# An expert layer's sorted rows: 32x32 block transposes on VectorE in place of TensorE transposes in the tile loop

## What is computed

```
router_logits = x @ router_w.T                 # [1024, 8]
topk_vals, topk_ids = top_k(router_logits, 1)
gate = sigmoid(topk_vals)
xs = x * gate
for e in 8 experts:                            # wg 256x1024, wd 512x256
    g, u = split(xs @ wg[e])
    o = (silu(g) * u) @ wd[e]
    routed += where(topk_ids == e, o, 0)
shared = silu_mul(x @ shared_gate_up) @ shared_down
out = routed + shared
```

## Time and profile before

| | |
|---|---|
| median of 3 runs | 129.22 us (129.17 to 129.29) |
| profiled execution, its own time | 129.24 us |
| its span in the trace | 127.6 us |
| PE busy, share of the span | 122.1 us, 96% |
| PE weight loads | 106.1 us, 83% |
| DVE busy | 79.4 us, 62% |
| ACT busy | 53.4 us, 42% |
| POOL busy | 35.4 us, 28% |
| granted TensorE clock | full in every slice |

### The profile page before, as it was taken

How to read it: one execution, slowest core, us unless ns; L and a number is a source line. 1 busy time by engine, 2 the same in 40 slices (tenths; PEclk the granted TensorE clock), 3 DMA queues, 4 the chain that set the end, 5 groups by cost and what they waited for, 6 DMA issues and landing times.

```text
span 127.6 us, 2426 instructions
## 1 busy us (share of the span) xinstructions
PE 122.1 (96%) x822; PEld 106.1 (83%) x822; DVE 79.4 (62%) x175; ACT 53.4 (42%) x113; POOL 35.4 (28%) x65
## 2 busy tenths in 40 slices
PE   4989999999999999999999999999999999999990
PEld 1248776788888857999999999999999978999990
DVE  0799695997899999875575553505040428922471
ACT  1678796829987546322222222242221337200000
POOL 7804040003879300040303030303030301687500
PEclk9999999999999999999999999999999999999999
DMA  3784999999993210129797989888982031033437
GB/s 83 207 281 37 330 360 244 181 207 397 385 380 136 82 51 0 46 81 318 264 321 258 295 275 277 307 280 303 281 303 63 9 86 51 13 89 104 112 101 244
DMA packets 15748, 25.02 MB, mean 196 GB/s; under 512 B 1296, under 2 KB 12632, under 8 KB 15736
## 3 DMA queue, kind: packets, MB, share of 16 engines
q1 hardware_dynamic: 13368, 20.66, 53.1%
q0 software_dynamic: 1456, 3.41, 8.2%
q10 hardware_dynamic: 912, 0.80, 1.9%
HBM read 18.78 MB, written 6.08 MB: 195 GB/s over the span
## 4 chain that ended last, share of the span: by engine, by line
PE 80%; POOL 6%; issue 5%; DMA 4%; DVE 2%; ACT 0%; DVEq 0%; POOLq 0%
PE ps L1112 25%; PE ps L1126 13%; PE ps L300 6%; POOL q_sb L458 6%; PE ps L302 5%; PE ps L301 5%; PE ps L975 5%; PE ps L988 4%; PE ps L981 4%; PE ps L1066 4%; DMA q_sb<-sorted_rows,slot_row 2%; PE ps L1053 2%; DMA sorted_rows<-yrow 2%; PE ps L1060 2%; DVE x_sb L895 1%
## 5 line engine op out<-in xcount | busy, mean ns | idle before, releaser
L1112 PE MATMUL ps<-xgT,gu 128*128 128x144 f32 x256 | 34.2, 287 | 0.0
L1112 PEld LDWEIGHTS ps<-xgT,gu 128*128 128x128 f32 x256 | 32.3, 190 | 0.5 <-issue 0.2
L826 DVE TENSOR_TENSOR wqkv<-rz,ps 128x288 f32<-128x288 f32 x16 | 7.3, 454 | 25.5 <-ACT rz L576 25.5
L440 POOL DMA_DIRECT2D sorted_rows<-yrow x9 | 5.0, 558 | 54.7 <-DVE yrow L821 54.7
L1126 PE MATMUL ps<-wqkv,dn 128*128 128x144 f32 x128 | 17.4, 289 | 0.0
L576 ACT ACTIVATE rz<-ps 128x288 f32<-128x288 f32 x16 | 6.5, 409 | 25.0 <-PE ps L1112 25.0
L1126 PEld LDWEIGHTS ps<-wqkv,dn 128*128 128x128 f32 x128 | 16.1, 190 | 0.0
L432 POOL DMA_INDIRECT sorted_rows<-xn,slot_row x8 | 9.8, 1220 | 15.4 <-ACT xn L514 13.6
L300 PE MATMUL ps<-xT_hi,sgu_hi 128*128 128x512 f32 x32 | 13.0, 407 | 0.0
L301 PE MATMUL ps<-xT_lo,sgu_hi 128*128 128x512 f32 x32 | 12.6, 394 | 0.0
L302 PE MATMUL ps<-xT_hi,sgu_lo 128*128 128x512 f32 x32 | 12.6, 394 | 0.0
(11 more groups left out here) (162 smaller groups left out, 231.3 us busy)
## 6 DMA issues: line engine op xcount, KB each, us to landing
gu<-in_L_ffn_w_gate_up_dram SPq DMA_DIRECT2D x8, 1024.0 KB
dn<-in_L_ffn_w_down_dram SPq DMA_DIRECT2D x8, 512.0 KB
sorted_rows<-zeros SPq DMA_DIRECT2D x1, 2592.0 KB, 18.0
wqkv<-sorted_rows SPq DMA_DIRECT2D x10, 144.0 KB
sorted_rows<-yrow POOLq DMA_DIRECT2D x9, 128.0 KB, 2.1
sgu<-_ffn_shared_gate_up_dram SPq DMA_DIRECT2D x1, 1024.0 KB, 6.2
wqkv<-in_L_attn_w_qkv_dram SPq DMA_DIRECT2D x3, 256.0 KB, 3.7
x_sb<-in_L_attn_x_dram SPq DMA_DIRECT2D x2, 256.0 KB, 3.6
```

Of the source, the lines that this page charges most:

```text
L826: V.tensor_tensor(hr[:, 2 * h:2 * h + 2, :].rearrange("p f s -> p (f s)"), act_sb[:, h, 0:2 * SLOTS], ps[:, 2 * h + 1, 0:2 * SLOTS], ALU.m ...
L1112: ins = mm(ps[:, 2 * h + u, (f % 2) * SLOTS:(f % 2 + 1) * SLOTS], gu[p][:, kc, col:col + P], xgT[:, kc, :], start=(kc == 0), stop=(kc == K ...
```

## The change

The sorted rows are loaded so that feature 2 f + c of a slot sits in partition f, by four DMAs, one for each 32 partitions, with runs of 64 floats (256 bytes). One DVE transpose in blocks of 32x32 (`sorted_in`) makes `xgT` of them, with the even features in one chunk and the odd ones in the other. The gate and up weights are therefore loaded with rows 2 p and 2 p + 1 in partition p (one run of 8 KB instead of two of 4 KB), and the down weights are read with a step of two floats. Another DVE transpose (`rows_out`) reads the down projection's PSUM and writes `yrow`, from which four DMAs store with runs of 256 bytes. Since a tile is now moved as 160 rows of which 144 are its own, a tile's stores must land before those of the next begin; POOL waits for that. Both kinds of PE transposes, ACT's copies of `xgT` and `yT`, and the two DVE copies are gone. The last tile's four stores are issued two by POOL and two by SP.

```diff
-        xg = early[0:HS, 0:2 * D].rearrange("p (j d) -> p j d", j=2)
+        xg = early[:, 0:NSQ * SQ * KC].rearrange("p (j f) -> p j f", j=NSQ)
...
-        gu_dram = w_gate_up.rearrange("e (c p) n -> e p c n", p=P)
+        gu_dram = w_gate_up.rearrange("e (p c) n -> e p c n", c=KC)
...
+        def row_store(eng, t, b, q, s_store):
+            rows = sorted_rows[bass.ds(t * SLOTS, NSQ * SQ), q * SQ * KC:(q + 1) * SQ * KC]
+            eng.dma_start(rows.rearrange("(j p) f -> p j f", p=SQ), yrow[q * SQ:(q + 1) * SQ, b, :, :]).then_inc(s_store, 16)
...
         # SP
-            def sorted_load(t):
-                sp.dma_start(xg, sorted_rows[bass.ds(t * SLOTS + SLOTS, SLOTS), :].rearrange("(j p) d -> p j d", p=HS)).then_inc(s_xg, 16)
+            def sorted_load(first, s_load):
+                for q in range(P // SQ):
+                    rows = sorted_rows[bass.ds(first, NSQ * SQ), q * SQ * KC:(q + 1) * SQ * KC]
+                    sp.dma_start(xg[q * SQ:(q + 1) * SQ, :, :], rows.rearrange("(j p) f -> p j f", p=SQ)).then_inc(s_load, 16)
...
-                    sp.wait_ge(s_xgT, t + 2)
-                    sorted_load(t + 2)
+                    sp.wait_ge(s_xgc, t + 2)
+                    sorted_load(t * SLOTS + 3 * SLOTS, s_xg)
...
         # POOL
-            for t in range(E - 1):
-                row_store(t, t % 2)
+            for t in range(1, E - 1):
+                pool.wait_ge(s_yrow, t + 1)
+                if t >= 2:
+                    pool.wait_ge(s_ystore, 64 * (t - 1))
+                for q in range(P // SQ):
+                    row_store(pool, t, (t - 1) % 2, q, s_ystore)
...
         # ACT
-                sorted_copy(t + 2, 4)
-                act.wait_ge(s_down, t + 1)
-                A(yT[:, 0:KC * P].rearrange("p (c s) -> p c s", c=KC), ps[:, 5:7, 0:P], ACT.Copy)
-                A(yT[:, KC * P:].rearrange("p (s c) -> p c s", c=KC), ps[:, 5:7, P:SLOTS], ACT.Copy).then_inc(s_yT, 1)
...
         # DVE
+            def sorted_in():
+                V.transpose(xgT[:, :, :], xg.rearrange("p j (f c) -> p c j f", c=KC)).then_inc(s_xgc, 1)
...
             for k in range(LAST):
+                if k == LAST - 1:
+                    dve.wait_ge(s_xg0, 64)
+                    sorted_in()
                 hidden(k)
...
+            def rows_out(t, b, stored):
+                dve.wait_ge(s_down, t)
+                if stored is not None:
+                    dve.wait_ge(s_ystore, stored)
+                V.transpose(yrow[:, b, :, :].rearrange("p j (f c) -> p c j f", c=KC), ps[:, 5:7, 0:NSQ * SQ]).then_inc(s_lastrow if t is total else s_yrow, 1)
...
+            def expert_tile(t, b=None, stored=None):
+                if b is not None:
+                    rows_out(t, b, stored)
                 for h in range(2):
                     dve.wait_ge(s_silu, 2 * t + (h + 1))
...
-                    if h == 0:
-                        rows_copy(t, b, stored)
+                dve.wait_ge(s_xg, 64 * t + 64)
+                dve.wait_ge(s_gup, 2 * t + 2)
+                sorted_in()
...
         # PE
                         ins.then_inc(s_gup, 1)
-                        if h == 0:
-                            pe.wait_ge(s_yrow, t + 1)
-                            transpose_back(t + 1)
+                    pe.wait_ge(s_yrow, t + 1)
                     if e == 0:
                         pe.wait_ge(s_sh, LAST)
-                    transpose_sorted(4, s_xg, 16 * t + 16)
...
-                                ins = mm(ps[:, 5 + c, 0:SLOTS], dn[p][:, f, c * P:(c + 1) * P], hr[:, f, :],
+                                ins = mm(ps[:, 5 + c, 0:SLOTS], dn[p][:, f, :].rearrange("p (m c) -> p c m", c=KC)[:, c, :], hr[:, f, :],
```

More of the change, by code:

```diff
@@ L19 @@
 SLOTS = 144
-HS = SLOTS // 2
-REST = SLOTS - 128
+SQ = 32
+NSQ = (SLOTS + SQ - 1) // SQ
 WARM = 14
@@ L138, in build @@
         dn = [sb(f"dn{p}", [P, FC, D], F32) for p in range(2)]
[L139 to L142, removed]
+        xgT = sb("xgT", [P, KC, NSQ * SQ], F32)
+        yrow = sb("yrow", [P, 2, NSQ, SQ * KC], F32)
         early = wqkv[:, :, :].rearrange("p c n -> p (c n)")
-        xg = early[0:HS, 0:2 * D].rearrange("p (j d) -> p j d", j=2)
+        xg = early[:, 0:NSQ * SQ * KC].rearrange("p (j f) -> p j f", j=NSQ)
         hr = early[:, 2 * D:2 * D + FC * SLOTS].rearrange("p (f s) -> p f s", f=FC)
@@ L266, in build @@
         s_down = sem("s_down")
-        s_yT = sem("s_yT")
-        s_yback = sem("s_yback")
         s_yrow = sem("s_yrow")
-        s_ystore = [sem(f"s_ystore{b}") for b in range(2)]
+        s_ystore = sem("s_ystore")
         s_stored = sem("s_stored")
-        s_lastrest = sem("s_lastrest")
-        s_restdone = sem("s_restdone")
+        s_lastrow = sem("s_lastrow")
+        s_ylast_sp = sem("s_ylast_sp")
+        s_ylast_pool = sem("s_ylast_pool")
         s_gather = [sem(f"s_gather{i}") for i in range(NT)]
@@ L368, in _ @@
                 rows_of(e)
-            sp.wait_ge(s_xg, 16 * ends[7] + 16)
-            sp.wait_ge(s_lastrest, 1)
-            sp.dma_start(sorted_rows[bass.ds(ends[7] * SLOTS + P, REST), :].rearrange("s (c d) -> (s c) d", c=KC), yrest[:, 0, :]).then_inc(s_restdone, 16)
+            sp.wait_ge(s_xg, 64 * ends[7] + 64)
+            sp.wait_ge(s_lastrow, 1)
+            sp.wait_ge(s_stored, 1)
+            for q in range(2, P // SQ):
+                row_store(sp, ends[7], 1, q, s_ylast_sp)
             for i in range(1, NT, 2):
@@ L436, in _ @@
             total = pool.value_load(plan[0:1, E - 1:E], min_val=E, max_val=TILES)
[L438 to L442, removed]
-            for t in range(E - 1):
-                row_store(t, t % 2)
-            with pool.Fori(E - 1, total) as t:
-                row_store(t, 1)
-            row_store(total, 0)
-            pool.wait_ge(s_qkv_sum, KC)
[L450 to L455, removed]
+            for t in range(1, E - 1):
[4 more added lines that the diff above has]
+                    row_store(pool, t, (t - 1) % 2, q, s_ystore)
+            with pool.Fori(E - 1, total) as t:
+                pool.wait_ge(s_yrow, t + 1)
+                pool.wait_ge(s_ystore, 64 * t - 64)
+                for q in range(P // SQ):
+                    row_store(pool, t, 0, q, s_ystore)
+                pool.wait_ge(s_ystore, 64 * t)
+            pool.sem_inc(s_stored, 1)
+            pool.wait_ge(s_lastrow, 1)
+            for q in range(2):
+                row_store(pool, total, 1, q, s_ylast_pool)
+            pool.wait_ge(s_qkv_sum, KC)
+            pool.wait_ge(s_ylast_pool, 32)
+            pool.wait_ge(s_ylast_sp, 32)
             for i in range(NT):
@@ L538, in _ @@
                         scale_tokens({8: range(0, 3), 9: range(3, NT)}[t])
-            def sorted_copy(done, bank):
-                act.wait_ge(s_xgT, done)
-                A(xgT[:, :, :], ps[:, bank, 0:KC * SLOTS].rearrange("p (c s) -> p c s", c=KC), ACT.Copy).then_inc(s_xgc, 1)
             def hidden_hi(k):
@@ L847, in first_tile @@
             def first_tile(t):
-                expert_tile(t, t % 2, 32 * (t // 2) if t >= 2 else None)
+                if t:
+                    expert_tile(t, (t - 1) % 2, 64 * (t - 2) if t >= 3 else None)
+                else:
+                    expert_tile(t)
             first_tile(0)
@@ L876, in _ @@
             with dve.Fori(E - 1, total) as t:
-                expert_tile(t, 1, 32 * t - 32 * (E // 2))
+                expert_tile(t, 0, 64 * t - 64)
+            rows_out(total, 1, 64 * (E - 2))
             attention(0)
-            rows_copy(total, 0, 32 * (E // 2), LAST_BACK)
             attention(1)
@@ L1112, in _ @@
                                     ins = mm(ps[:, 2 * h + u, (f % 2) * SLOTS:(f % 2 + 1) * SLOTS],
-                                             gu[p][:, kc, col:col + P], xgT[:, kc, :], start=(kc == 0), stop=(kc == KC - 1))
+                                             gu[p][:, kc, col:col + P], xgT[:, kc, 0:SLOTS], start=(kc == 0), stop=(kc == KC - 1))
                         ins.then_inc(s_gup, 1)
-                        if h == 0:
-                            pe.wait_ge(s_yrow, t + 1)
-                            transpose_back(t + 1)
+                    pe.wait_ge(s_yrow, t + 1)
                     if e == 0:
                         pe.wait_ge(s_sh, LAST)
-                    transpose_sorted(4, s_xg, 16 * t + 16)
                     pe.wait_ge(s_dn[p], 16 * (e // 2) + 16)
@@ L1147, in _ @@
             pe.wait_ge(s_xgc, total + 1)
-            pe.wait_ge(s_yrow, total + 1)
             spread_reciprocals()
```

41 lines of the change are left out of this document (6 added, 35 removed).

## The result

| | before | after |
|---|---|---|
| median | 129.19 us (128.99 to 129.29, 4 runs) | 131.79 us (131.24 to 132.38, 4 runs) |
| ratio, 95% interval | | 1.0204 (1.0158 to 1.0250) |
| profiled execution, its span | 129.24, 127.6 | 131.77, 130.1 |

Slower by 2.6 us. Forecast were 133.3 us, in a range of 127.8 to 137.0. Executions over 1.5% above the fastest of their kernel are left out of all medians and ranges here: one each of `gu_4k`, `pitch160`, `xg_two` and `xg_two_head`, two of four each of `in_only` and `head_early`.

A forecast was written before the change was run, and what follows sets the result against it. PE was taken to bound the turn, with weight refills already on the edge of the critical path. 129.24 + 0.9 (ahead of the loop) + 3.8 (late refill) - 0.65 (behind it) = 133.3 us, range 127.8 to 137.0.

The forecast's parts named there:

- The refill: Tile loop: `gu` issued 3.6 us behind T0 (end of gate and up matmuls), so PE waits: +3.8 us; chance 0.60.
- the formula of the text: Tile loop, two turns: refill issue behind T0, issue to use, gate and up: 3.6 + 6.9 + 3.91 = 14.41 us.
- My two ends: Refill's issue to use: 6.2 us from a load outside the loop, 7.65 from a late one; 6.9 taken.
- Turns without a hold: Tile loop: a turn nothing else holds takes 6.18 us, 0.34 less than before, the down matmuls' second half awaiting products.
- Ahead of the loop: First tile: `sorted_in` stands behind a scan and `hidden_lo`, start 1.55 us later; term to T0 of tile 1 +0.9.
- Behind the loop: After the last T0: spread reached in 2.27 us, not 2.48, and the last turning back (0.45) goes: -0.65.
- Stores: Tile loop: four issues of 0.56 us and a 2.1 us landing finish before the next; nothing waits: 0.
- The transposes: DVE: each 320-element transpose takes 0.47 us at one element per cycle, bounds 0.40 and 1.52.
- The rival of slow transposes: DVE: transposes take 1.52 us each, `gu` is issued 1.05 later: +4.2, 137.5 us; chance 0.08.
- The strided weights: Down matmuls: weights read with a step of two keep the pace of contiguous reads: 0, at worst 1.95 us a tile.
- Short runs: DMA engines: 256-byte packets fill them; at 42 ns each, issue to use grows by 1.3: 137.2 us; chance 0.07.
- Refills in time: Tile loop: issue to use under 4.9 us, so refills hold no turn: 127.2 us, faster; chance 0.20.

The follow-up runs named there:

- `gu_4k`: Changed kernel with the gate and up weights loaded in two runs of 4 KB instead of one of 8 KB: 131.45 us.
- `pitch160`: Changed kernel with tiles 160 rows apart in `sorted_rows`, so POOL waits for no earlier stores in the loop: 132.55 us.
- `xg_two`: Changed kernel with two buffers of sorted rows, a tile's row loads issued behind `dn`, two turns ahead of use: 129.39 us.
- `xg_two_head`: `xg_two` with the first `sorted_in` also moved up on DVE, ahead of the scan and `hidden_lo`: 128.54 us.
- `in_only`: Kernel before with only the row-loading half: four short loads and `sorted_in`, results turned back and stored as before: 132.72 and 133.82 us.
- `head_early`: Changed kernel with the first `sorted_in` moved ahead of the scan and `hidden_lo` on DVE: 131.06 and 132.17 us.
- experiment 1: Changed kernel with SP issuing the refill of `gu` ahead of the four loads of sorted rows: 132.85 us.
- `before_split4`: Kernel before with its one row load per tile split in four of 18 partitions, same 1 KB runs: 131.07 us.
- `out_only`: Changed kernel with only the result half: `rows_out` and four short stores, rows loaded and transposed as before: 126.24 us, again 126.23.
- experiment 5: Changed kernel with two buffers of sorted rows, then also the first `sorted_in` moved up: 129.39 and 128.54 us.
- experiment 3: Kernel before with its row load split in four, by partitions with 1 KB runs or by columns with 256-byte runs: 131.07 and 131.22 us.
- `gu_first`: Changed kernel with the refill of `gu` issued ahead of the four row loads on SP's queue: 132.85 us.
- `loads_act`: Changed kernel with the four loads of sorted rows issued on ACT's queue, behind its second silu: 132.79 us.

## Why the prediction was right, and where it was off

**The refill**, +3.8 forecast, +1.5 measured. The mechanism is the one told: idle ahead of tiles 2, 3, 5, 6 and 7 that ends with `gu`, which experiment 1 took away. The size was wrong: L, issue to use, was taken at 6.9 us with 6.2 as the low end, and it was 5.75. The issue came 4.0 behind T0, not 3.6, since SP began the row loads at T0 + 1.83, not 1.7, and the four took 1.86, not 1.65. The two errors offset in part: over three pairs the shorter L takes 3.5 us off and the later issue adds 1.2. By the formula of the text, 4.0 + 5.75 + 3.91 is 13.66 for two turns and 41.0 for three pairs, against 40.89 measured. The result lies in the range, but at the low end (131.2) of what the text gave for this case by itself.

Why L was short: it is no constant. Where PE waited for `gu`, the refill was issued 0.3 us behind T0 in `xg_two` (69.01, used at 77.54: L 8.53), 1.4 behind in the kernel before (L 7.47 and 7.65), 2.8 in `before_split4` (64.21 to 70.83: 6.62), 4.0 in the changed kernel (5.75). T0 to use comes to 8.85, 8.95, 9.42 and 9.73: an issue 3.7 us later lands 0.9 later. So at least 2.8 of the 8.5 us were waiting, and what is issued later waits less. That it waits behind other transfers is argued, not shown; the DMA engines are 70 to 90% busy or more in every slice from 61.8 to 100.8 us of the changed kernel (40 slices of 3.25 us, in tenths):

```profile
DMA  3783999999997220203898887799889243033327
```

My two ends came from a load outside the loop and from two within it that were issued early; neither was a bound for an issue at another time. The time from T0 to use is no constant either: 9.2 to 10.4 over the five tiles of the changed kernel. Three refills lie outside even that: 11.5 us in `head_early`, 11.3 and 12.2 in `pitch160`. Why isn't shown.

**Turns without a hold**, 6.18 forecast: 6.15 (52.65 to 58.80), with the wait for the products between the halves of the down matmuls as told (0.22 of idle). `out_only` shows the other side of the same step: that wait was room for the transposes.

**Ahead of the loop**, +0.9 forecast, +1.3 measured. The first tile begins 2.0 later, not 1.55; in the other kernels with the transpose in that place it began at 51.99 to 52.54, so 1.3 to 1.9 is the place, and the rest varies from one execution to the next.

**Behind the loop**, -0.65 forecast, -0.3 measured. The turning back is gone, but T0 to the spread stayed at 2.46. The last rows weren't in place sooner. In the kernel before, POOL's last store and the first gather:

```profile
106.30 0.55 POOL L440 DMA_DIRECT2D sorted_rows<-yrow  x1 [4.23 <-DVE yrow L821]
109.23 1.53 POOL L458 DMA_INDIRECT q_sb<-sorted_rows,slot_row  x1 [2.38 <-POOLq L454]
```

and in the changed kernel POOL's two stores, SP's two and the first gather:

```profile
107.88 1.20 POOL L302 DMA_DIRECT2D sorted_rows<-yrow  x2 [2.25 <-DMA sorted_rows<-yrow]
109.17 0.90 SPq L302 DMA_DIRECT2D sorted_rows<-yrow  x2
112.42 1.43 POOL L462 DMA_INDIRECT q_sb<-sorted_rows,slot_row  x1 [3.33 <-DMA sorted_rows<-yrow]
```

The first gather starts 8.45 us behind the last T0 before and 8.81 now. POOL's share goes out earlier behind T0 (4.27, not 5.52), but SP's 5.56 behind it, 2.5 us after `rows_out`. In the code SP first waits for the row loads of a tile that isn't there. In `pitch160`, which lacks the wait for earlier stores, it is 2.5 us too; in `xg_two`, where no such loads are on their way then, SP's share goes out 0.24 us after `rows_out`.

**Stores**, 0 forecast. "Nothing waits" was wrong, and its time nearly right: stores land in 4.5 us, not 2.1, POOL waits for them 25.4 us in six waits and `rows_out` 3.9 in two. That POOL waits was named as a sign of being wrong, and it came true; but in the loop these waits lie beside the wait for `gu`, and `pitch160` wins nothing by taking POOL's away. They are the next bound, as experiment 5 shows.

**The transposes.** 0.47 us each forecast. Groups of the changed kernel by shape:

```profile
L791 DVE STREAM_TRANSPOSE xgT<-wqkv 128x320 f32<-128x320 f32 x9 | 4.5, 504 | 0.0
L818 DVE STREAM_TRANSPOSE yrow<-ps 128x320 f32<-128x320 f32 x8 | 4.1, 510 | 4.3 <-DMA sorted_rows<-yrow 3.9 <-PE ps L1106 0.3
```

Blocks of 32x32 with reads (`sorted_in`) or writes (`rows_out`) two floats apart run within 0.04 us of the 0.47 worked out from plain copies, from SBUF as from PSUM. The rival of slow transposes falls.

**The strided weights**, 0 forecast: loads of down weights take 196 ns in the mean beside 190 for gate and up, and 190 for contiguous down weights in the kernel before, but all 16 of a tile take 2.03 us in `out_only`, which reads them strided too, and took 2.02 before.

```profile
L1106 PEld LDWEIGHTS ps<-wqkv,dn 128*128 128x128 f32 x128 | 16.8, 196 | 1.8 <-DVE wqkv L825 1.8
```

That is the rule cited from the Trainium skill, *SBUF — State Buffer*, cachelines; the trace agrees.

**Short runs.** The rival falls too. A packet of 256 bytes took 18 ns in the median in the trace of the changed kernel, one of 1 KB 46; the dear end of the text was 42. Runs of 256 bytes cost 0.15 us more than runs of 1 KB (experiment 3), and the fastest kernel of all stores in them. The Trainium skill, *DMA: Bandwidth & Descriptors*, Specifications, sets the loss below 512 bytes; if stores lose by it, it didn't reach the time here. What hurts is the number of DMAs to issue and where they stand.

**Refills in time** had a chance of 0.20 and falls for this change. For half of it, it came true, with 126.2 us.

## What to carry to other kernels

A change with two halves is to be costed, and tried, as two: here one half was worth -2.8 us and the other cost +4.2, and together they cost more than the sum, because a turn that waits for weights doesn't pass on what is saved in it. Before work is taken off an engine, look for what would fill its place; transposes that lie in a wait for another engine are free, and four DMAs in place of one on the queue that also carries the weights are not. And the time from a DMA's issue to its use holds only for an issue at that time: where part of it is waiting, a later issue shortens it, and the time of use behind a fixed event (here T0) is the better number to carry over, with a spread of 1 us here.

## What the runs showed of the hardware

PE's clock fell after two waits of some 2.2 us, and after others of like length it didn't. In `gu_first` PE stood idle for 2.23 us ahead of tile 3, in `xg_two` for 2.20 in tile 7; the windows of 1 us of `xg_two` there (columns: the window; its length and the busy time and count of PE, PEld, DVE, ACT and POOL; granted clock, DMA share, GB/s):

```profile
101.00:102.00 1.00, 0.00 (x0) 0.00 (x0) 0.70 (x2) 0.00 (x0) 0.00 (x0) 1.00 0.00 0
102.00:103.00 1.00, 0.79 (x4) 0.80 (x5) 0.93 (x3) 0.00 (x0) 0.37 (x1) 0.76 0.02 8
103.00:104.00 1.00, 1.00 (x6) 1.00 (x5) 0.00 (x0) 0.00 (x0) 0.88 (x3) 0.50 0.23 41
104.00:105.00 1.00, 1.00 (x6) 1.00 (x5) 0.00 (x0) 0.00 (x0) 0.94 (x2) 0.50 0.24 41
105.00:106.00 1.00, 1.00 (x5) 0.82 (x4) 0.00 (x0) 0.00 (x0) 0.09 (x1) 0.54 0.46 82
```

A clock of 0.50 is 1.2 GHz. The 16 weight loads of that down projection took 3.62 us and not 2.03, and the gate and up of tile 3 in `gu_first` 5.64 and not 3.97: a wait of 2.2 us cost some 1.6 us more behind it. In `xg_two_head` a wait of 2.31 us, in `head_early` one of 2.23, in `loads_act` one of 1.94 and in `pitch160` one of 2.71 were followed by the full clock, so the length of the wait alone doesn't decide. What does isn't shown.

The whole time of `xg_two` shows it: of the eleven executions counted, four had a mean clock of 0.987 and took 130.30 to 131.04 us, the other seven, at 0.999 or 1.000, took 129.10 to 129.79. The profiled one had 0.987, too, and took 131.15. In `gu_first` it doesn't show: the profiled execution (0.986) took 132.73 us, the three at the full clock 132.17 to 133.33. Waits of this length can thus add to the time or to its spread by more than themselves, and don't always.
